# Second attention: the head sums are written into the rows of their values, and ScalarE normalises the next tiles

## The reference, cut to what matters

```
x = x + tanh(g_xattn[0]) * memory_attention(layernorm(x), ctx, mask)            # one head
x = x + tanh(g_ffn[0])   * ffn_1bit(layernorm(x), w1, w2, w3)                   # quantised
x = x + tanh(g_xattn[1]) * attention_16_heads(layernorm(x), ctx, mask, Wq .. bo) # changed here
x = x + tanh(g_ffn[1])   * (silu(h @ Wg.T) * (h @ Wu.T)) @ Wd.T,  h = layernorm(x)

attention_16_heads:                # head width 16, 128 queries and 128 keys a batch
  q, k, v = proj(h, Wq), proj(ctx, Wk), proj(ctx, Wv)
  s       = clip(where(attend, q k / 4, -1e4), -50, 50)
  p       = softmax(s);  o = p v
  delta   = layernorm(rs * (o Wo + bo)) * gamma + beta
```

## Time and profile before

| what | value |
|---|---|
| time, median of 3 runs (lowest to highest) | 244.17 us (243.62 to 246.03) |
| the profiled execution: its own time, its span | 244.73 us, 242.9 us |
| busy share of the span: PE, PEld, DVE, ACT, POOL | 89%, 73%, 64%, 56%, 52% |
| stage C on PE: first and last `head_sums` start at | 116.82 us, 166.12 us |
| mean granted clock of TensorE | 0.972 of full speed |

### The profile page before, as it was taken

The page is one execution under the profiler, slowest core; times in us unless marked ns, Lnnn a source line. Parts: engine busy times, 40 slices in busy tenths (PEclk is TensorE's granted clock), DMA queues, the critical chain, the costliest instruction groups (busy, mean ns, idle before and its releaser), DMA issues. The chain is left out here.

```text
span 242.9 us, 5228 instructions
## 1 busy us (share of the span) xinstructions
PE 217.0 (89%) x1960; PEld 176.7 (73%) x1960; DVE 155.4 (64%) x391; ACT 135.3 (56%) x288; POOL 125.3 (52%) x202
## 2 busy tenths in 40 slices
PE   8399997989999899866999999979989999999992
PEld 7266565768877687754878778767868888888872
DVE  1775788678899999826457777785563432444233
ACT  2132888687887788794667877544342322323230
POOL 3546363867887876645847777797379100000000
PEclk9959997999999999999999999979999999999999
DMA  4999203650000000000000000000000000020002
GB/s 137 366 400 369 60 3 88 258 173 3 0 1 0 3 1 0 3 0 0 3 3 5 3 4 3 3 3 0 3 0 0 3 1 0 0 89 0 0 0 86
DMA packets 9576, 12.59 MB, mean 52 GB/s; under 512 B 1104, under 2 KB 8016, under 8 KB 9552
## 3 DMA queue, kind: packets, MB, share of 16 engines
q1 hardware_dynamic: 9120, 12.07, 14.3%
q10 hardware_dynamic: 432, 0.20, 0.4%
HBM read 11.22 MB, written 1.05 MB: 50 GB/s over the span
## 5 line engine op out<-in xcount | busy, mean ns | idle before, releaser
L1467 PE MATMUL PB<-SGN,WHI 128*128 128x512 f32 x128 | 41.8, 408 | 0.0
L814 DVE TENSOR_TENSOR QM<-SIL,PB 128x512 f32<-128x512 f32 x16 | 11.0, 688 | 33.5 <-ACT SIL L1140 33.5
L1140 ACT ACTIVATE SIL<-PB 128x512 f32<-128x512 f32 x16 | 9.6, 599 | 36.4 <-PE PB L1467 36.4
L1467 PEld LDWEIGHTS PB<-SGN,WHI 128*128 128x128 f32 x128 | 23.9, 195 | 4.6
L1484 PE MATMUL PB<-WHI,SGN 128*128 128x256 f32 x128 | 25.7, 284 | 1.4 <-DVE SGN L822 1.4
L1270 PE MATMUL PB<-SGN,XQH 128*128 128x512 f32 x64 | 26.2, 409 | 0.0
L1467 PE MATMUL PB<-SGN,WLO 128*128 128x512 f32 x64 | 25.7, 402 | 0.0
L1270 PE MATMUL PB<-SGN,XQL 128*128 128x512 f32 x64 | 25.6, 400 | 0.0
L440 POOL TENSOR_TENSOR HBQ<-HB,HSD 128x512 f32<-128x512 f32 x16 | 16.7, 1045 | 15.4 <-ACT HB L1047 15.3
L1088 ACT ACTIVATE HBQ<-PB 128x512 f32<-128x512 f32 x32 | 17.5, 613 | 10.8 <-PE PB L1409 10.8
L337 POOL TENSOR_TENSOR RSTD<-MVS,MHALF 128x1 f32<-128x1 f32 x24 | 14.5, 605 | 16.3 <-DVE MVS L538 16.3
(11 more groups left out here) (140 smaller groups left out, 557.5 us busy)
## 6 DMA issues: line engine op xcount, KB each, us to landing
WRAW<-w_dram SPq DMA_DIRECT2D x3, 1024.0 KB, 10.9
WRAW<-w_dram SPq DMA_DIRECT2D x1, 2048.0 KB, 7.4
X<-x_dram SPq DMA_DIRECT2D x2, 512.0 KB, 7.0
CTXT<-ctxt_dram SPq DMA_DIRECT2D x2, 512.0 KB, 8.2
CTX<-ctx_dram SPq DMA_DIRECT2D x2, 512.0 KB, 9.2
WRAW<-wd_dram SPq DMA_DIRECT2D x1, 1024.0 KB, 5.6
out_dram<-X SPq DMA_DIRECT2D x4, 256.0 KB, 2.5
WQK<-wqkvo_dram SPq DMA_DIRECT2D x1, 512.0 KB, 10.8
```

Of the source, the lines that this page charges most:

```text
L814: nc.vector.tensor_tensor(GU[:, b, :], SG[:, b, :], PB[2 * b + 1][:], ALU.mult).then_inc(d_g, 1)
L1467: mm = nc.tensor.matmul(PB[2 * b + m][:], wcol(w_part, m, c, j), act_part[:, c, g * TG:(g + 1) * TG], start=(c == 0 and i == 0), stop=(c = ...
```

## The change

`SEL` becomes two matrices of width 32 with 16 columns of ones each. `head_sums` is 16 products of 128 columns: each writes the sum of a head 16 times, into the rows that the head's values have in `PB[6]`. So the sums are a 128 x 256 block in `PB[7]`, laid out as the values; the reciprocal covers 256 columns in place of 64, and `OT` is its product with `PB[6]` as it stands. `SPREAD`, `spread_sums`, `values_out` and their semaphores go. `xd_t` now waits for `OT` (`c_o`) where it waited for `values_out` (`c_pc`); the next `head_sums` waits for the reciprocal, and the next `head_values` for `OT`.

The `norm` of stage C moves from DVE to ACT (`norm_c`): in stage C's step `t` behind `q_out(t+1)`, for tiles 0 and 1 at the end of stage B's steps 6 and 7. It needs the offset, so POOL runs `x_offset` for each tile behind its `rstd`: in stage B's steps 3 to 7, and for the last three tiles between the stages.

Cut to its core, the diff shows in this order: the setup on POOL; POOL in stage B; DVE in stage B and in stage C; `norm_c` and its places on ACT in stages B and C; `head_sums`, `head_values`, `spread_sums`, `xd_t` and the loop of stage C on PE.

```diff
-            for r in range(2 * CT4):
-                nc.gpsimd.memset(SEL[:, r, r:r + 1], 1.0).then_inc(set_pool, 1)
-            nc.gpsimd.memset(SEL[:, 0, 2 * CT4:], 1.0).then_inc(set_pool, 1)
+            for e in range(2):
+                nc.gpsimd.memset(SEL[:, e, e * HD:(e + 1) * HD], 1.0).then_inc(set_pool, 1)
...
                 if live(t - 3):
                     rstd(t - 3, t - 3 + NT)
+                    x_offset(t - 3, t - 3 + NT)
...
-                if t >= 6:
-                    norm(t - 6, t - 6, 2)
...
                     dve.wait_ge(c_dn, t)
-                    nc.vector.reciprocal(RD[:], PB[7][:, 0:P // 2]).then_inc(c_rd, 1)
-                if live(t + 2):
-                    norm(t + 2, p, 2)
+                    nc.vector.reciprocal(RD[:], PB[7][:, 0:D]).then_inc(c_rd, 1)
                 if live(t - 3):
                     norm_d(t - 3)
                 if t == NT:
                     lo_gu(0)
                 if live(t - 1):
-                    dve.wait_ge(c_sp, t)
-                    dve.wait_ge(c_pc, t)
-                    nc.vector.tensor_tensor(OT, PV, PB[7][:, D:2 * D], ALU.mult
-                                            ).then_inc(c_o, 1)
+                    dve.wait_ge(c_rd, t)
+                    dve.wait_ge(c_pv, t)
+                    need(dve, c_dl, t - 1)
+                    nc.vector.tensor_tensor(OT, RD[:], PB[6][:, 0:D], ALU.mult).then_inc(c_o, 1)
...
+            def norm_c(t, p):
+
+                act.wait_ge(nm_x, 2 * (NT + t) + 2)
+                need(act, xt_done, 2 * NT + t - 1)
+                nc.scalar.activation(XH[:, p, :], X[:, t, :], ACT.Identity,
+                                     bias=NMB[:, t:t + 1], scale=RSTD[:, t:t + 1]
+                                     ).then_inc(ln_done, 1)
...
+                if t >= 6:
+                    norm_c(t - 6, t - 6)
...
-            def values_out(u):
-                act.wait_ge(c_pv, u + 1)
-                need(act, c_o, u)
-                nc.scalar.copy(PV, PB[6][:, 0:D]).then_inc(c_pc, 1)
...
                     q_out(t + 1)
+                if live(t + 2):
+                    norm_c(t + 2, p)
                 if live(t - 2):
                     centred(t - 2)
-                if live(t - 1):
-                    values_out(t - 1)
...
                 pe.wait_ge(c_p, u + 1)
+                need(pe, c_rd, u)
                 for c in range(DC):
                     for e in range(2):
-                        for half in range(2):
-                            r = (2 * c + e) * 2 + half
-                            for j in range(CT4):
-                                at = head_at(HPC * c + 2 * j + e) + half * (P // 2)
-                                mm = nc.tensor.matmul(
-                                    PB[7][HB32 * j:HB32 * (j + 1), 0:P // 2], SEL[:, r, :],
-                                    PR[:, p, at:at + P // 2], start=(r == 0),
-                                    stop=(r == 2 * CT4 - 1))
+                        for j in range(CT4):
+                            at = head_at(HPC * c + 2 * j + e)
+                            mm = nc.tensor.matmul(
+                                PB[7][HB32 * j:HB32 * (j + 1), c * P:(c + 1) * P], SEL[:, e, :],
+                                PR[:, p, at:at + P], start=(e == 0), stop=(e == 1))
                 mm.then_inc(c_dn, 1)
...
             def head_values(u, p):
                 pe.wait_ge(c_v, 2 * u + 2)
-                need(pe, c_pc, u)
+                need(pe, c_o, u)
...
-            def spread_sums(u):
-
-                pe.wait_ge(c_rd, u + 1)
-                for k in range(2 * DC):
-                    at = D + k * (P // 2)
-                    mm = nc.tensor.matmul(PB[7][:, at:at + P // 2], SPREAD[:, k, :], RD[:],
-                                          start=True, stop=True)
-                mm.then_inc(c_sp, 1)
...
             def xd_t(u):
                 pe.wait_ge(d_ln, u + 1)
-                pe.wait_ge(c_pc, min(u + 3, NT))
+                pe.wait_ge(c_o, min(u + 3, NT))
...
                     head_values(t - 1, 1 - p)
-                if live(t - 1):
-                    spread_sums(t - 1)
```

More of the change, by code:

```diff
@@ L172, in gated_block @@
         V1 = sb("V1", [P, 2, NH, HB32])
-        SEL = sb("SEL", [P, 2 * CT4, HB32])
-        SPREAD = sb("SPREAD", [P, 2 * DC, P])
+        SEL = sb("SEL", [P, 2, HB32])
         VA = CTX
@@ L179, in gated_block @@
         PR = HBQ[:].rearrange("p (b a) n -> p b (a n)", b=2)
-        RD = sb("RD", [P, P // 2])
+        RD = sb("RD", [P, D])
         C_OUT = HB[:].rearrange("p b g s -> p (b g s)")[:, 0:6 * D].rearrange("p (k n) -> p k n",
                                                                               k=6)
-        OT, DL, XD, PV, D1, D2 = (C_OUT[:, k, :] for k in range(6))
+        OT, DL, XD, D1, D2 = (C_OUT[:, k, :] for k in range(5))
         HTH = SGN[:, 0, :].rearrange("p (c n) -> p c n", c=DC)
@@ L237, in gated_block @@
         set_a = sem("set_a")
-        set_spread = sem("set_spread")
         set_c = sem("set_c")
@@ L260, in gated_block @@
         (c_kv, c_ko, c_vo, c_v, c_ht, c_q, c_qm, c_s, c_ex, c_p, c_dn,
[L261 removed]
+         c_pv, c_rd, c_o, c_dl, c_de, c_st, c_mv, c_nm, c_ve, c_r2, c_of, c_d1, c_d2,
          c_xb) = (
             sem("c_" + n) for n in ("kv", "ko", "vo", "v", "ht", "q", "qm",
[L264 removed]
+                                    "s", "ex", "p", "dn", "pv", "rd", "o", "dl", "de",
                                     "st", "mv", "nm", "ve", "r2", "of", "d1", "d2", "xb"))
@@ L355, in norm_a, with x_offset @@
                                         ).then_inc(ln_done, 1)
-            def x_offset(t):
+            def x_offset(t, m):
                 nc.gpsimd.tensor_tensor(NMB[:, t:t + 1], MVS[:, t, 0:1], NEG1[:], ALU.mult
                                         ).then_inc(nm_x, 1)
-                pool.wait_ge(nm_x, 2 * t + 1)
-                pool.wait_ge(rstd_ready, t + 3)
+                pool.wait_ge(nm_x, 2 * m + 1)
+                pool.wait_ge(rstd_ready, m + 3)
                 nc.gpsimd.tensor_tensor(NMB[:, t:t + 1], NMB[:, t:t + 1], RSTD[:, t:t + 1],
                                         ALU.mult).then_inc(nm_x, 1)
[L366 to L371, removed]
             x_groups = [P, D // GS, GS]
@@ L405, in step_a @@
                     rstd(t - 2, t - 2)
-                    x_offset(t - 2)
+                    x_offset(t - 2, t - 2)
             half_rstd(0)
@@ L414, in _ @@
                 step_a(t, t % 2)
-            pool.wait_ge(ld["ident"], 16)
-            for c in range(DC):
-                for half in range(2):
-                    spread_rows(c, half)
             def halves(buf, p, half):
@@ L507, in _ @@
             rstd(NT - 3, 2 * NT - 3)
+            x_offset(NT - 3, 2 * NT - 3)
             quantised_h(NT - 1, 1, 1)
@@ L513, in _ @@
             rstd(NT - 2, 2 * NT - 2)
+            x_offset(NT - 2, 2 * NT - 2)
             rstd(NT - 1, 2 * NT - 1)
+            x_offset(NT - 1, 2 * NT - 1)
             w_lo_slice(0)
@@ L1156, in _ @@
                 if n == 0:
-                    values_out(NT - 1)
                     hi_d(NT - 3)
@@ L1168, in _ @@
             pe.wait_ge(ld["ident"], 16)
-            pe.wait_ge(set_pool, 2 * CT4 + 5)
+            pe.wait_ge(set_pool, 6)
             def transpose_x(src, bank, done):
```

1 line of the change is left out of this document (removed).

## The result

The changed kernel takes 248.46 us, the median of 20 runs (245.99 to 250.1), beside 245.09 us of the kernel before in its 20 (243.5 to 249.03): a ratio of 1.0137, 95% interval 1.0105 to 1.017. Slower by 3.4 us, where I forecast 1.2 us faster, and outside my range. The profiled execution took 245.99 us, span 244.2, the quickest of the 20; its mean granted clock was 0.965 (before: 0.972 in 244.73 us), that of the others 0.945 to 0.965. (Ratios are taken over undisturbed executions, so they aren't quite those of the medians.)

The account below looks back on a forecast made before the run. PE, and from step 3 a loop through `spread_sums`, ACT and DVE, was taken to bound stage C. Terms -4.7 + 0.8 + 1.7 + 1.0 = -1.2 took 244.17 to 243.0 us, range 240.6 to 245.6.

Parts of the forecast that it names:

- stage B later: Stage B: `x_offset` on POOL ahead of `quantised_h` costs 0.40 us in each of steps 4 and 5, +0.8 us.
- gain up to `gate_up_d(0)`: Stage C: 2.1 us saved in steps 1 and 2, 3.1 in steps 3 to 6, +0.5 in the last, together -4.7.
- tail: Step after stage C: `xd_t(5)` and `gate_up_d(1)` wait for `OT(7)` behind the wide reciprocal, +1.7 us.
- low clock in `gate_up_d(1)`: Tail: new PE idle time brings a second stretch at granted 0.50, costing 0 to 1.75 us, taken as +1.0.
- the reciprocal's price from two rows: DVE: a straight line through the reciprocals of 64 and 1 columns gives 1.77 us for 256 columns.
- PE's step: Stage C: without `spread_sums` and with the wider `head_sums`, PE needs 5.56 us a step instead of 6.59.
- DVE as the next bound: Stage C: DVE's loop takes 6.08 us a step, more than PE's 5.56, so DVE is late next.
- `lo_d` free of ACT: Stage C on DVE: `lo_d` no longer waits for ACT, where it had waited 1.03 us.
- the idle time ahead of `xd_t(5)`: Last attention step: PE stands idle about 3 us ahead of `xd_t(5)`, with granted clock 0.50 in `gate_up_d(1)` after.
- The second rival: DVE: the reciprocal takes up to 2.21 us, counted six times, making the kernel slower at 245.6 us; chance 0.10.
- the third: Stage C: `norm` ahead of the exponentials on ACT keeps steps 3 to 6 at 6.6 us, 245.0 us; chance 0.13.
- The first rival: Tail: no second low clock stretch, 242.0 us, or none at all, 240.2 us; chance 0.27.

Follow-up runs that it names:

- Holding POOL: Changed kernel with POOL's product with `GAM` in stage C held until `norm_d` of the step has ended: 244.87 us, ratio 0.9967 to the kernel before.
- filler: Changed kernel with useless matrix products on PE in its waits ahead of `xd_t(4)` and `xd_t(5)`: 243.23 us, ratio 0.9933 to the kernel before.
- control of both gates early: Kernel before, with the `gate_up_d(0)` and `gate_up_d(1)` products moved ahead of `xd_t(4)` and `xd_t(5)`: 247.8 us, ratio 1.0113.
- both gates early: Changed kernel with `gate_up_d(0)` ahead of `xd_t(4)` and `gate_up_d(1)` ahead of `xd_t(5)` on PE: 238.15 us, ratio 0.9717 to the kernel before.
- normalisation only: Kernel before with only stage C's `norm` moved to ACT and `x_offset` on POOL; sums, spread and values' copy as before: 246.87 us, ratio 1.008.
- four edits: Changed kernel with both gate products early, POOL's `GAM` product held, stage B's offsets put later, also the last behind `quantised_h(7,1)`: 239.15 us, ratio 0.9757.
- sums only: Changed kernel with stage C's `norm` back on DVE and without POOL's offset products in stage B: 248.98 us, ratio 1.0105 to the kernel before.
- the last three versions: Changed kernel with gate products early, `GAM` product held, offsets late (0.9736); last offset late too (0.9757); also `lo_gu(0)` behind `OT(7)` (0.9695).
- `gate_up_d(1)` early: Changed kernel with `gate_up_d(1)` ahead of `xd_t(5)` on PE in the last attention step: 243.06 us, ratio 0.9868 to the kernel before.
- narrow reciprocal: Changed kernel with the reciprocal over only the first 64 of 256 columns, the others set to 1.0: 241.03 us, ratio 0.9856 to the kernel before.
- before with filler: Kernel before with 6 useless matrix products on PE ahead of `spread_sums` of step 7: 243.88 us, ratio 0.9947.

## Why the prediction was wrong, step by step

Against the profiled execution of before, from the rows:

| step | forecast | profiled |
|---|---|---|
| stage B later | +0.8 | +0.96 (`transpose_hq(7,1)` at 108.35, 107.39) |
| gain up to `gate_up_d(0)` | -4.7 | -3.4 |
| tail | +1.7 | +2.6 |
| low clock in `gate_up_d(1)` (and 0.1 less in `gate_up_d(0)`) | +1.0 | +1.1 |
| sum | -1.2 | +1.3 |

- **Right:** the reciprocal's price from two rows (1.77, measured 1.75); PE's step, 5.54 us twice; DVE as the next bound; `lo_d` free of ACT; the idle time ahead of `xd_t(5)` and the granted 0.50 behind it. The second rival, a dearer reciprocal, and the third, ACT holding the step, both fell, though the kernel did turn out slower, as each would have had it.
- **`norm_d` beside POOL is the step that failed in the traces.** I took 0.32 us for `norm_d` from the row of the `norm`, which ran while POOL was in `rstd`, an instruction of one column. The row of `norm_d` itself in that step already showed 0.41, beside another product of POOL:

```profile
145.22 0.62 POOL L337 TENSOR_TENSOR RSTD<-MVS,MHALF 128x1 f32<-128x1 f32 x1
145.74 0.94 POOL L472 TENSOR_TENSOR V<-CTX,BV 128x128 f32<-128x128 f32 x2
145.95 0.41 DVE L829 TENSOR_SCALAR HB<-X,MVS,RSTD 128x256 f32<-128x256 f32 x1
...
175.26 0.68 DVE L822 TENSOR_TENSOR SGN<-QM,SGN 128x512 fp32r<-128x512 f32 x1
175.42 0.93 POOL L483 TENSOR_TENSOR RSTD<-VE,MHALF 128x1 f32<-128x1 f32 x1 [4.04 <-DVE VE L881]
```

In the changed kernel it met POOL's products on SBUF and took 0.75, in the tail 1.16. That is 0.4 in each of three steps and 0.8 in the tail, most of what the gain and the tail fell short by. Holding POOL gave back about half of it in a step and all of it in the tail. `lo_gu` had shown the same before: 1.25, and 0.68 at 175.26 with a single column on POOL. The Trainium skill, SBUF — State Buffer (SBUF: two separate sides), says that VectorE and GpSimd share one pair of ports under a lock, which a VectorE operation takes when it uses both ports or reads two inputs from SBUF: the one that starts first has the pair for its whole instruction, and the other blocks meanwhile. The trace agrees in the main: `norm_d` ends at 145.06, 0.15 us after POOL's product. Not all of its own 0.32 came after that, and beside `rstd` (145.22 to 145.84) the `norm` took no more than 0.32, where by that rule it would have waited.
- **The clock's price is the term that was mis-sized most, by the medians.** I priced one more low stretch, from one execution, at 1.0. In the profiled execution it came out so (+1.1), but that one is the quickest of the 20. Over all runs the filler gives back 5.2 us of the median in the changed kernel and 1.4 in the kernel before. If that is all clock, its price is 3.8 instead of 1.0, and 2.8 of the 4.6 us by which I missed; the traces show 2.7 of the 5.2, and the mean clocks (0.945 to 0.965 without the filler, 0.970 to 0.984 with it) speak for the rest. My evidence against a fall, a wait of 1.90 us without one, was a single row, and it didn't hold: with the same program up to there, a wait of 1.91 us was followed by 0.50 in the control of both gates early (its row stands at the end). The first rival, no second low stretch, lay on the wrong side.
- **Stage B came out near for other reasons.** By the place of the earlier trace rows, which is the second half of tile 4, it is 1.09 us later (84.41 to 85.50, the wait there 1.05 instead of 0.64), not 0.8: 0.4 in each of steps 4 and 5 as forecast, and 0.23 in step 3, which I had put at nothing because PE was full. Then 0.54 came back, as DVE lost its `norm` in step 6 (`transpose_hq(6,1)` follows 3.76 us after the one before it, 4.30 before). And 0.40 was added by `norm_c` on ACT, which I had costed at nothing: from `transpose_hq(7,0)` to `(7,1)` it is 5.21 us with it (normalisation only, four edits), 4.81 without (before, sums only).

## What to carry to other kernels

Where one engine becomes the bound, ask what the former one does meanwhile: TensorE's waits ahead of wide products (2.7 and 3.8 us) came to cost more here than the work saved was worth, and filling them with work that is ready, by order alone, turned a loss of 1.4% into a gain of 3%. Don't take the price of a VectorE operation on SBUF from a row in which GpSimd is silent, or the price of the clock from one execution.

## What the runs showed of the hardware

- The same wait of 2.3 us ahead of `transpose_hq(7,1)` was followed by a granted 0.50 between 107 and 115 us in five profiled runs (normalisation only, both gates early, the last three versions) and by 1.00 in five others (the changed kernel, `gate_up_d(1)` early, POOL's product held, filler, narrow reciprocal). The shorter wait at that place in the kernel before, 1.9 us, was followed by 1.00 in three runs (before, before with filler, sums only) and by 0.50 in one, the kernel before with both gates early:

```profile
108.49 0.65 PE L1298 MATMUL PB<-ident,HBQ 128*128 128x128 f32 x4 [1.91 <-POOL HBQ L440]
109.00:113.00 4.00, 3.73 (x20) 3.44 (x19) 1.36 (x4) 1.44 (x4) 0.81 (x2) 0.57 0.00 0
```

After waits of 2.7 us ahead of `xd_t(4)` `gate_up_d(0)` ran at 0.50 in the changed kernel, and at full clock in the run with the sums alone. The length of the wait didn't decide it; what did stays open.
- The mean clock of the changed kernel's runs goes from 0.965 down to 0.945, their time from 246 up to 250 us; where in those runs the low stretches lay wasn't seen, only that the filler in two places raises the whole range, to 0.970 to 0.984.
